# The first self attention's output product as three products of rounded halves

## The reference, cut to what matters

```
scores = einsum('bhtd,bsd->bhts', q, k1) * scale      # causal mask
probs  = softmax(scores)
attn   = einsum('bhts,bsd->bhtd', probs, v1)
out    = transpose(attn, (0, 2, 1, 3)).reshape(B, T, H * D)
return out @ Wo.T                                     # the product that changes
```

## Time and profile before

| | |
|---|---|
| median of three runs | 1902.81 us |
| the profiled execution's own time | 1893.62 us |
| its span (first to last instruction) | 1891.8 us |
| mean granted TensorE clock, share of full | 0.96 |
| stage of the change, first transposes of p to last update | about 99 to 229 us |

### The profile page before, as it was taken

The page is one execution under the profiler, slowest core; times in us unless marked ns, Lnnn a source line. Parts: engine busy times, 40 slices in busy tenths (PEclk is TensorE's granted clock), DMA queues, the critical chain, the costliest instruction groups (busy, mean ns, idle before and its releaser), DMA issues. The chain is left out here.

```text
span 1891.8 us, 32666 instructions
## 1 busy us (share of the span) xinstructions
PE 1716.8 (91%) x10942; PEld 1357.1 (72%) x10942; DVE 1013.6 (54%) x2460; ACT 773.8 (41%) x2128; POOL 657.6 (35%) x551
## 2 busy tenths in 40 slices
PE   4889779999999999999999879999889799886898
PEld 3767567777777777777777668899677566654666
DVE  4456465556565656555656424332462566646664
ACT  1266334444444444444544412343114576631210
POOL 0022225445555555545555523343500223343000
PEclk9989989999999999999999969999989899997999
DMA  3000040000000000000000034853300000010000
GB/s 93 0 1 0 18 151 11 10 9 0 9 9 9 9 9 9 9 9 9 0 9 9 1 89 157 261 190 121 93 19 1 1 0 0 0 55 1 0 20 20
DMA packets 48468, 67.19 MB, mean 36 GB/s; under 512 B 11762, under 2 KB 42706, under 8 KB 45714
## 3 DMA queue, kind: packets, MB, share of 16 engines
q1 hardware_dynamic: 46866, 62.66, 10.7%
q0 software_dynamic: 1536, 3.67, 0.6%
HBM read 57.02 MB, written 9.31 MB: 35 GB/s over the span
## 5 line engine op out<-in xcount | busy, mean ns | idle before, releaser
L580 POOL TENSOR_SCALAR l0x_p<-l0x_p,l0x_inv 112x488 f32<-112x488 f32 x256 | 386.4, 1521 | 376.5 <-DVE l0x_inv L670 376.5
L765 ACT ACTIVATE l0x_p<-l0x_s,l0x_low 112x488 f32<-112x488 f32 x256 | 178.4, 697 | 292.2 <-DVE l0x_low L659 281.4
L659 DVE CUSTOM_DVE_ANT_0 l0x_s<-l0x_score_ps,l0x_bias 112x488 f32<-112x488 f32 x256 | 160.3, 664 | 137.8 <-PE l0x_score_ps L904 127.8
L912 PE MATMUL l0x_pT_ps<-ident,l0x_p 112*122 112x112 f32 x1024 | 126.4, 264 | 15.1 <-POOL l0x_p L580 15.1
L646 DVE TENSOR_TENSOR l0x_kT_lo<-l0x_proj_ps,l0x_kT_hi 128x488 fp32r<-128x488 f32 x128 | 85.3, 666 | 100.0 <-ACT l0x_kT_hi L755 100.0
L925 PE MATMUL l0x_oT_ps<-l0x_pT,l0x_v 122*64 122x112 f32 x2048 | 127.5, 267 | 9.8 <-ACT l0x_pT L771 6.1
L912 PEld LDWEIGHTS l0x_pT_ps<-ident,l0x_p 112*122 112x122 f32 x1024 | 108.5, 140 | 38.5 <-POOL l0x_p L580 23.6
L925 PEld LDWEIGHTS l0x_oT_ps<-l0x_pT,l0x_v 122*64 122x64 f32 x2048 | 100.2, 137 | 49.1 <-issue 34.1
L1773 POOL TENSOR_TENSOR l1a_pn<-l1a_p,l1a_inv 112x1792 f32<-112x1792 f32 x16 | 50.9, 3182 | 206.5 <-DVE l1a_inv L1800 206.5
L1846 ACT ACTIVATE l1a_p<-l1a_p,l1a_shift 112x112 f32<-112x112 f32 x256 | 95.3, 373 | 62.6 <-DVE l1a_shift L1794 62.6
L860 PE MATMUL l0x_proj_ps<-l0x_kvT_hi,l0x_wkv_hi 128*128 128x488 f32 x256 | 110.7, 432 | 3.6 <-DVE l0x_kvT_lo L627 3.6
(11 more groups left out here) (347 smaller groups left out, 3778.8 us busy)
## 6 DMA issues: line engine op xcount, KB each, us to landing
l0f_w<-in_l0f_w SPq DMA_DIRECT2D x21, 1024.0 KB, 4.7
l0x_c_in<-in_ctx SPq DMA_DIRECT2D x16, 375.0 KB
l0f_context<-in_ctx SPq DMA_DIRECT2D x16, 375.0 KB
sorted_x<-l0x_zeros SPq DMA_DIRECT2D x1, 2816.0 KB, 21.1
l0f_xs<-sorted_x SPq DMA_DIRECT2D x21, 128.0 KB, 2.2
sorted_y<-l0f_ys SPq DMA_DIRECT2D x21, 128.0 KB, 1.7
l0x_wkv<-in_l0x_wkv SPq DMA_DIRECT2D x2, 1024.0 KB, 10.3
x<-in_x SPq DMA_DIRECT2D x1, 1792.0 KB, 9.6
```

Of the source, the lines that this page charges most:

```text
L580: nc.gpsimd.tensor_scalar(p[:, i % 2, a, :], p[:, i % 2, a, :], inv[:, i % 2, a:a + 1], None, ALU.mult).then_inc(pn_ready, 1)
L659: nc.vector.tensor_tensor_reduce(s_sb[:, h % 2, :], score_ps[0:S, h % 2, 0:KEYS], bias[:], -SCALE, 3.4e38, ALU.add, ALU.min, low[:, h:h + ...
L765: nc.scalar.activation(p[:, h // 2 % 2, h % 2, :], s_sb[:, h % 2, :], ACT.Exp, scale=-1.0, bias=low[:, h:h + 1], accum_out=total[:, h:h + ...
L912: done = nc.tensor.transpose(pT_ps[0:KT, a, t * S:(t + 1) * S], p[:, i % 2, a, t * KT:(t + 1) * KT], ident[0:S, 0:S])
```

## The change

`wo` is split once at the start of the stage: ScalarE rounds it into `wo_hi` (after `take_queries(0)`, ahead of the first exponentials), VectorE subtracts to get `wo_lo` (after `softmax(0, 0)`), and TensorE waits for that before its loop. Per batch, `copy_o` now writes the rounded `oT_hi` and raises `o_hi_ready`; VectorE's new `split_o` waits for it, subtracts `oT_hi` from `o_ps` into `oT_lo`, and raises `o_ready`, on which TensorE's product waits as before. In VectorE's order `split_o(g, 0)` stands behind `invert_sums(g, 1)` and ahead of `softmax(g + 1, 0)`, and `split_o(g, 1)` at the end of the step. The product of each head becomes three. The first phase's other parts and all other phases stay as they are.

```diff
--- before.py
+++ after.py
@@ -123,13 +123,15 @@
     with ExitStack() as ctx:
         ph = Phase(nc, ctx, "l0a")
         wo = ph.sb("wo", [128, H, D])
+        wo_hi, wo_lo = ph.sb("wo_hi", [128, H, D], F32R), ph.sb("wo_lo", [128, H, D], F32R)
         pos_q, pos_k = ph.sb("pos_q", [DH, S]), ph.sb("pos_k", [DH, 1])
         causal = ph.sb("causal", [S, S])
         mv, half, rstd = ph.sb("mv", [S, B, 2]), ph.sb("half", [S, B]), ph.sb("rstd", [S, B])
         all_qT, qT = ph.sb("all_qT", [DH, H, B * S]), ph.sb("qT", [DH, H, PAIR])
         kT = ph.sb("kT", [DH, B * S])
         all_v, v = ph.sb("all_v", [S, B, DH]), ph.sb("v", [S, 2, DH])
-        pT, oT = ph.sb("pT", [S, H, S]), ph.sb("oT", [DH, 2, H, S])
+        pT, oT_hi = ph.sb("pT", [S, H, S]), ph.sb("oT_hi", [DH, 2, H, S], F32R)
+        oT_lo = ph.sb("oT_lo", [DH, 2, H, S], F32R)
         top, shift = ph.sb("top", [S, 2, H]), ph.sb("shift", [S, 2, H])
         total, inv = ph.sb("total", [S, 2, H]), ph.sb("inv", [S, 2, H])
         x_new, x_stats = ph.sb("x_new", [S, D]), ph.sb("x_stats", [S, 6])
@@ -143,6 +145,7 @@
         qv_ready, x_w, stats_done = ph.sem("qv_ready"), ph.sem("x_w"), ph.sem("stats_done")
         score_done, softmax_step, exp_ready = ph.sem("score_done"), ph.sem("softmax_step"), ph.sem("exp_ready")
         pn_ready, pT_done, pT_ready = ph.sem("pn_ready"), ph.sem("pT_done"), ph.sem("pT_ready")
+        wo_hi_ready, wo_lo_ready, o_hi_ready = ph.sem("wo_hi_ready"), ph.sem("wo_lo_ready"), ph.sem("o_hi_ready")
         o_done, o_ready, y_done, x_step = ph.sem("o_done"), ph.sem("o_ready"), ph.sem("y_done"), ph.sem("x_step")
 
 
@@ -335,12 +338,21 @@
                         nc.vector.tensor_copy(pT[:, 4 * a:4 * a + 4, :].rearrange("p h s -> p (h s)"),
                                               score_ps[0:S, 2 * j + a, 0:4 * S]).then_inc(pT_ready, 1)
 
+                def split_o(g, j):
+                    b = g * 2 + j
+                    dve.wait_ge(o_hi_ready, b + 1)
+                    nc.vector.tensor_tensor(oT_lo[:, j].rearrange("p (a h) s -> p a (h s)", a=2), o_ps[:, :, 0:4 * S],
+                                            oT_hi[:, j].rearrange("p (a h) s -> p a (h s)", a=2).bitcast(F32), ALU.subtract
+                                            ).then_inc(o_ready, 1)
+
                 def update(g, j):
                     b = g * 2 + j
                     dve.wait_ge(y_done, b + 1)
                     update_x(nc, dve, x, stats, x_new, x_stats, y_ps[0:S, j, 0:D], b, x_step)
 
                 softmax(0, 0)
+                dve.wait_ge(wo_hi_ready, 1)
+                nc.vector.tensor_tensor(wo_lo[:], wo[:], wo_hi[:].bitcast(F32), ALU.subtract).then_inc(wo_lo_ready, 1)
                 invert_sums(0, 0)
 
                 def body(g, first, last):
@@ -349,12 +361,14 @@
                     if not first:
                         update(g - 1, 1)
                     invert_sums(g, 1)
+                    split_o(g, 0)
                     if not last:
                         softmax(g + 1, 0)
                     copy_pT(g, 1)
                     update(g, 0)
                     if not last:
                         invert_sums(g + 1, 0)
+                    split_o(g, 1)
                 over_steps(dve, body, G)
                 update(G - 1, 1)
 
@@ -379,10 +393,11 @@
                     b = g * 2 + j
                     act.wait_ge(o_done, b + 1)
                     since(act, y_done, b - 1)
-                    nc.scalar.activation(oT[:, j].rearrange("p (a h) s -> p a (h s)", a=2), o_ps[:, :, 0:4 * S],
-                                         ACT.Copy).then_inc(o_ready, 1)
+                    nc.scalar.activation(oT_hi[:, j].rearrange("p (a h) s -> p a (h s)", a=2), o_ps[:, :, 0:4 * S],
+                                         ACT.Copy).then_inc(o_hi_ready, 1)
 
                 take_queries(0)
+                nc.scalar.activation(wo_hi[:], wo[:], ACT.Copy).then_inc(wo_hi_ready, 1)
                 exp(0, 0)
 
                 def body(g, first, last):
@@ -433,8 +448,10 @@
                     pe.wait_ge(o_ready, b + 1)
                     since(pe, x_step, b * 4 - (7 if j == 0 else 3))
                     for c in range(H):
-                        done = nc.tensor.matmul(y_ps[0:S, j, 0:D], oT[:, j, c, :], wo[:, c, :],
-                                                start=(c == 0), stop=(c == H - 1))
+                        nc.tensor.matmul(y_ps[0:S, j, 0:D], oT_hi[:, j, c, :], wo_hi[:, c, :], start=(c == 0), stop=False)
+                        nc.tensor.matmul(y_ps[0:S, j, 0:D], oT_hi[:, j, c, :], wo_lo[:, c, :], start=False, stop=False)
+                        done = nc.tensor.matmul(y_ps[0:S, j, 0:D], oT_lo[:, j, c, :], wo_hi[:, c, :],
+                                                start=False, stop=(c == H - 1))
                     done.then_inc(y_done, 1)
 
                 def body(g, first, last):
@@ -452,6 +469,7 @@
 
                 score(0, 0)
                 score(0, 1)
+                pe.wait_ge(wo_lo_ready, 1)
                 over_steps(pe, body, G)
                 project_out(G - 1, 1)
     return ph.sems
```

## The result

The changed kernel takes 1909.82 us (median of 12 runs, 1906.61 to 1913.56), the kernel before, timed beside it, 1902.72 us (12 runs). The ratio is 1.0037 with a 95% interval of 1.0028 to 1.0047: slower by 7.1 us. Two later sets of runs gave 1.0036 [1.0023, 1.0050] and 1.0033 [1.0023, 1.0042]. The forecast was 1906.1 us, +3.3, in a range of 1899.5 to 1913.0. The time is in the range and the mechanism holds, but the outcome that had been called likeliest (within 0.2%, chance 0.50) didn't come: slower by over 0.2% had 0.41. The size forecast is about half of what was measured.

The account below looks back on a forecast made before the run. TensorE bounds the whole program; in this stage the chain of 8.13 us sets the period. Terms −0.65, +3.0 and +0.96 give +3.3 us on the median 1902.81: 1906.1 us, range 1899.5 to 1913.

Parts of the forecast that it names:

- The product: Output product in each batch: 24 rounded records 0.117 us apart, 2.81 us instead of 3.46, 0.65 us less on PE.
- Rival 1: Output product: a fixed cost of short rounded products, c = 0.123 us, +5.5 us in all; chance 0.23 including its slow form.
- estimated by interpolation: Output product's record spacing at 256 columns from the skill page's 131 and 81 ns: 98 ns, sum −4 us.
- The split: VectorE's subtraction between copy and product: 1.09 us plus 0.04 handover from ACT, 1.13 us added to the path.
- the sum: Whole stage: batch 0 −0.65, batches 1 to 13 +3.0, batches 14 and 15 +0.96, together +3.3 us.
- What comes late: Full batches: chain 8.13 us against 7.90 sets the period, PE idles about 0.9 us; work queued behind split_o stays covered.
- The bare chain: Transposes to transposes where no score is left, batches 14 and 15: 8.13 us against 7.65 before.
- The start of the stage: Rounding wo on ACT, 1.91 us, and subtracting wo_lo, 2.29 us, fall in idle time and cost nothing.
- Batch 0: First batch: scores at the lower clock end after the subtraction, PE doesn't wait, gain of 0.65 us.
- rival 3: PE's clock falls from 0.9 us of idle a batch; 2.9 us per slow batch, five make +14 us; chance 0.05.
- The very slow form of rival 1: Output product: weight load and stream don't overlap, c = 0.216 us, +41 us, 1944 us; chance 0.05.
- rival 2: Subtraction hidden before the product, PE keeps −10.5 us, 1892.3; milder form a faster stream, 1899; chance 0.09.

Follow-up runs that it names:

- c8: The changed kernel a third time, no edit, as control on the same chip as c9: 1910.12 us, ratio 1.0033 to the kernel before.
- c10: The kernel before, unedited, looked at once more on the same chip as c8: profiled span 1899.4 us.
- c0: The changed kernel run again without edit, as control of its set: 1899.64 us against 1892.55 before, ratio 1.0036.
- c1: Changed kernel with the sixteen products of rounded values issued first, only the eight remainder products waiting for the subtraction: 1884.97 us against 1892.55 before.
- c3: c1 with ScalarE's copy between the sixth and seventh exponential and split_o ahead of invert_sums: 1882.26 us against 1892.55 before, ratio 0.9941.
- c4: The kernel before, unrounded product kept, with only VectorE's subtraction added in the path before the product: 1921.88 us against 1904.71 before.
- c7: Changed kernel with each product cut into two of 128 columns, 48 records a batch: 1938.02 us, measured once.
- c5: Changed kernel with unread score products keeping TensorE busy during the last step's wait: 1910.00 us against 1904.71 before, ratio 1.0035.
- c9: The same edit as c5, run again on the same chip as c8: 1907.75 us against 1903.54 before, ratio 1.0021.

## Why the prediction was right, and what it under-counted

- **The product.** The forecast spacing of records was c = 0.117 us, measured 0.118; 24 records and the start take 2.92 us for 2.90. The weight load stayed hidden, as the prediction took it. Rival 1's fixed cost (0.123) isn't there. Nor is the 0.098 us that the prediction had estimated by interpolation. The Trainium skill ("TensorE: Matmul & The Clock Gate", "Back-to-back issue gap") gives a sustained spacing of 131 ns at 512 columns. This case's traces lie above it, with 0.232 us at 512 columns, and above the estimate with 0.118 us at 256.
- **The split.** It took 1.09 us and 0.03 of handover from ACT, for 0.04 forecast. From DVE to PE the sum took over the handover from copy to product that stands in its 4.10 us. In the written-out last step that holds (219.35 + 1.09 to 220.50: 0.06); in the looped batches the subtraction of 153.73 ends at 154.82 and the product starts at 154.96, 0.14 later. This is one term that was mis-sized: the chain is 8.21 us and not 8.13, and 13 batches cost 4.0 and not 3.0 us. Why the loop adds 0.08 wasn't tried.
- **What comes late.** The bare chain came out at 8.16 for 8.13. VectorE, ScalarE and GpSimd behind `split_o` cost nothing, as said: the transposes follow the product with no idle. The start of the stage costs nothing either (first transposes at 98.33 in c8, at 98.50 in c10).
- **Batch 0.** The prediction had it gain 0.65 us, since its scores ran at the lower clock and covered the subtraction. That depends on when the clock rises, which differs from trace to trace of one kernel. Where the granted clock over 80 to 106 us is 0.74, the batch goes from 10.77 us (the first trace of before) to 10.15 (c0), and TensorE doesn't wait: the gain is there. Where it is 0.80, it goes from 9.82 (c10) to 9.99 (c8): the scores end sooner, TensorE waits 0.56 us, and 0.2 us are lost. The first trace of the changed kernel is of the second kind.
- **The clock.** This is the larger term, which the sum put at nothing: it had the granted clock at 1.00 from 106 us on. The prediction priced rival 3 for full batches with their 0.9 us of idle and called it small. The clock held there in every trace (the rows show 0.56 to 0.72 us of idle). It fell where no score stands: there the idle is 1.01 + 1.13, measured 2.13 us, two times close together. The 1.13 was in the sum, but what 2.13 us of idle do to the clock wasn't asked. Each product hit costs 1.5 us, one of them in two of the three traces of this kernel and both in the third.

Together: 4.0 in the full batches, 1.1 in the last two without the lapse, 1.5 to 3.0 for the lapse and −0.6 to +0.2 in batch 0 are 6 to 8 us, against 7.1 measured. The forecast's direction rests on the mechanism, which the runs confirm. That the measured time also fell in the range is in part luck: the range had been made wide for rival 1's slower product, and it was the clock and the handover that used it. The very slow form of rival 1 and rival 2's hidden subtraction didn't come; most of what rival 2 would have paid (−10.5 us) is what c1 and c3 get by another order (−7.6 and −10.3).

## What to carry to other kernels

A faster product is worth what its own chain leaves of it: if the operands' new preparation ends later than the work that used to cover it, compare the two chains (here 7.90 us of TensorE's own order against 7.65 + 1.13 − 0.65 = 8.13) before counting the engine's busy time. Where a product is cut into parts, issue the parts first whose operands are ready first, and let only the last ones wait; here the same instructions went from +7 to −7.6 us by that, and to −10.3 with ScalarE's and VectorE's orders mended too. Ask of a new idle not only how long it is, but whether it stands in the unlooped ends, where nothing covers it and the clock may fall.

## What I had not expected of the hardware

- Rounded products of 256 columns come every 0.118 us (the changed kernel), which is 0.011 above 256 / 2.4 GHz; the excess at 448 columns (0.203) is 0.016, at 512 (0.232) 0.019. It grows with the columns, 9 to 10% in these three rows.
- Where TensorE idled 2.13 us before each of the last two products, the granted clock was at 1.2 GHz for part of the second product (the first trace of the changed kernel and c8: 0.21 us a record) or of both (c0 and c4), but of neither in c7 (1.00), whose products are longer. In the thirteen full batches, with some 0.7 us of idle each, and in c5 and c9, with 0.56 us in the last step, it stayed at 2.4 GHz. So the same idle can cost a lapse or not; what decides between one, two and none wasn't tried.
